# A four-layer graph network on one core: eight blocks' sums placed by node instead of by feature, and a third gathered tile in every run

## The reference, cut to what matters

```python
for l in range(4):
    m = relu(x[src] + (edge_weight @ We[l] + be[l]))       # one row of 512 per edge
    agg = segment_sum(m, dst, 1250)
    h = ((1 + eps[l]) * x + agg) @ W1[l] + b1[l]
    h = relu(batchnorm(h) * gamma[l] + beta[l])            # mean and variance over the nodes
    x = relu(h @ W2[l] + b2[l])
out = layernorm(x0 + x)
```

## Time and profile before

| | us |
|---|---|
| median of 3 runs | 1293.48 |
| lowest, highest | 1288.86, 1293.76 |
| profiled execution | 1292.47 |
| its span, first to last instruction | 1290.6 |
| PE busy | 1208.2 (94%) |
| DVE busy | 1035.8 (80%) |
| POOL busy | 783.6 (61%) |
| ACT busy | 553.5 (43%) |

### The profile page before, as it was taken

One profiled execution on the slowest core, in us unless ns is written; L12 is line 12 of the kernel. 1 busy time (PEld: TensorE's weight loads), 2 busy tenths in 40 slices (PEclk: granted clock), 3 DMA queues, 4 the chain that ended last, 5 costly groups with the idle time before them and its releaser, 6 DMA issues.

```text
span 1290.6 us, 26518 instructions
## 1 busy us (share of the span) xinstructions
PE 1208.2 (94%) x7483; PEld 771.6 (60%) x7483; DVE 1035.8 (80%) x2134; ACT 553.5 (43%) x1159; POOL 783.6 (61%) x831
## 2 busy tenths in 40 slices
PE   2887999999999999999998999999998999999997
PEld 2884566666655566666654566665554566666653
DVE  7978888888876978887776978887767888888777
ACT  1923344434364444434355444444345434343343
POOL 0055677677706777777715777777714777777720
PEclk9558899999999999999999999999999999999999
DMA  3156677677736777777746777777745777777752
GB/s 113 56 186 194 193 205 218 197 209 211 232 111 200 216 218 216 217 217 218 235 136 199 215 217 217 217 217 217 234 146 185 215 217 217 218 216 215 221 190 107
DMA packets 92578, 254.23 MB, mean 197 GB/s; under 512 B 19902, under 2 KB 23114, under 8 KB 92428
## 3 DMA queue, kind: packets, MB, share of 16 engines
q0 software_dynamic: 65600, 215.01, 56.5%
q1 hardware_dynamic: 25804, 36.42, 8.6%
q10 hardware_dynamic: 1024, 1.05, 0.3%
HBM read 239.24 MB, written 12.97 MB: 195 GB/s over the span
## 4 chain that ended last, share of the span: by engine, by line
POOL 42%; PE 29%; issue 15%; DVE 10%; DMA 2%; ACT 0%; ACTq 0%; DVEq 0%; POOLq 0%
POOL rows L827 42%; PE y_ps L2106 10%; PE y_ps L1985 6%; PE pair_ps L1932 4%; DVE rows L1543 3%; DVE rows L1429 2%; PE h_ps L2063 1%; PE y_ps L2117 1%; DMA rows<-node_table,src_fast 1%; PE h_ps L1858 1%; DVE src_onehot L1360 1%; PE uT_ps L2016 1%; DMA node_table<-rows 1%; PE pair_ps L2049 1%; PE uT_ps L2023 1%
## 5 line engine op out<-in xcount | busy, mean ns | idle before, releaser
L827 POOL DMA_INDIRECT rows<-node_table,src_fast x820 | 780.9, 952 | 453.3 <-issue 248.2
L1543 DVE SCALAR_TENSOR_TENSOR rows<-We_ps,negw_fast,rows 128x512 f32<-128x512 f32 x820 | 566.3, 744 | 81.6 <-DMA rows<-node_table,src_fast 81.2
L1985 PE MATMUL y_ps<-table_parts,src_onehot 128*128 128x512 f32 x1664 | 428.7, 409 | 22.0 <-DVE table_parts L637 8.0
L1985 PEld LDWEIGHTS y_ps<-table_parts,src_onehot 128*128 128x128 f32 x1664 | 291.3, 190 | 191.2 <-issue 88.0
L1003 ACT ACTIVATE rows<-y_ps 128x512 f32<-128x512 f32 x416 | 248.7, 598 | 217.7 <-PE y_ps L1985 207.2
L1932 PE MATMUL pair_ps<-rows,onehot 128*32 128x512 f32 x2504 | 306.2, 601 | 15.0 <-DVE rows L1543 14.8
L1360 DVE TENSOR_TENSOR src_onehot<-y_ps,src_bc 126x256 fp32r<-126x256 f32 x376 | 150.8, 417 | 64.2 <-PE y_ps L1985 63.9
L1932 PEld LDWEIGHTS pair_ps<-rows,onehot 128*32 128x32 f32 x2504 | 67.4, 109 | 149.5 <-issue 112.2
L2063 PEld LDWEIGHTS h_ps<-uT,W_sb 128*128 128x128 f32 x1152 | 135.5, 194 | 6.1 <-issue 3.4
L2063 PE MATMUL h_ps<-uT,W_sb 128*128 128x128 f32 x1152 | 136.4, 278 | 0.0
L2106 PE MATMUL y_ps<-rows,hT 128*128 128x512 f32 x288 | 124.5, 594 | 0.0
(11 more groups left out here) (251 smaller groups left out, 793.3 us busy)
## 6 DMA issues: line engine op xcount, KB each, us to landing
late_rows<-node_table SPq DMA_DIRECT2D x1536, 2.0 KB
rows<-node_table,src_fast POOLq DMA_INDIRECT x820, 3.7
b_bc<-node_table ACTq DMA_DIRECT2D x512, 2.0 KB
node_table<-rows SPq DMA_DIRECT2D x29, 256.0 KB, 3.6
src_onehot<-near_ws SPq DMA_DIRECT2D x416, 2.0 KB
x_now<-x_pad SPq DMA_DIRECT2D x10, 512.0 KB, 7.7
W_sb<-W SPq DMA_DIRECT2D x4, 1024.0 KB, 5.5
rows<-W SPq DMA_DIRECT2D x16, 256.0 KB
```

The source lines that it names most:

```text
L827: nc.gpsimd.indirect_dma_start(rows[:, slot, :], None, table[:, :], bass.IndirectOffsetOnAxis(src_fast[:, t:t + 1], 0)).then_inc(landed[q] ...
L1543: last = nc.vector.scalar_tensor_tensor(rows[:, slot, :], We_ps[:, :], negw_fast[:, t:t + 1], row, ALU.mult, ALU.max)
L1985: last = nc.tensor.matmul(y_ps[k % 2][:, :], src_onehot[:, 2 * (k % ONEHOTS) + b, :], table_parts[:, part, 2 * pair_of(k) + b, :], start=( ...
```

## The change

Two things. First, for blocks 0 to 7 (`BY_NODE` = 8) the sums are placed by node: the placing one-hot is the weight, in pieces of 128x32, and all 512 columns of `pair_sb` or `carry` stream through (`place_block`, six matmuls, five in block 0), at quad 1 where the old placing stood. VectorE adds the result to `u` (`add_sums`, after its messages of quad 3), and TensorE transposes the whole `u` (`turn_block`, after the sums of quad 3). ScalarE's copies move: `keep_carry` after `block_placed`, `finish_block` after `turn_block`, `scale_u` from before the near tiles to the middle of them. `place_w` of layer 0 moves from quad 1 to quad 2. Blocks 8 and 9 are placed as before.

Second, `EXTRA_RUNS[1]` takes every fourth run from 7 on instead of every eighth from 11, so that all later runs have three near tiles: 108 tiles a layer instead of 104 (one more in steps 1, 3, 5 and 7), and 20 extras instead of 16 at the start. `ln_stats` and `ln_mv` become parts of `stats`.

```diff
-    EXTRA_RUNS = [slice(LONG_A_STEP + 1, LONG_RUNS, LONG_A_STEP), slice(2 * LONG_A_STEP + 3, LONG_RUNS, 2 * LONG_A_STEP)]
-    TWO_RUNS = slice(LONG_A_STEP + 3, LONG_RUNS, 2 * LONG_A_STEP)
+    EXTRA_RUNS = [slice(LONG_A_STEP + 1, LONG_RUNS, LONG_A_STEP), slice(LONG_A_STEP + 3, LONG_RUNS, LONG_A_STEP)]
...
             def scale_u(n, i):
-                if n:
-                    act.wait_ge(u_turned, n)
+                if i == BLOCKS - 1:
+                    act.wait_ge(u_turned, n // BLOCKS * (BLOCKS - BY_NODE) + i - BY_NODE)
+                elif n:
+                    act.wait_ge(block_summed, n + 1)
...
                         act.wait_ge(We_rows, 64 * (l + 1))
+                    if 0 < i <= BY_NODE:
+                        act.wait_ge(block_placed, BY_NODE * l + i)
+                        keep_carry()
                     if 0 < i:
                         finish_block(n - 1)
-                        nc.scalar.copy(carry[:, :], pair_sb[:, 1, :]).then_inc(carry_copied, 1)
-                    if i < BLOCKS - 1:
+                    if i > BY_NODE:
+                        keep_carry()
+                    if i == 0:
                         scale_u(n, i)
                     copy_pair(0, n, quad_summed[3], n + 2)
                     for q in range(0 if i else 3, 4):
                         make_tiles(l, first + q)
+                        if q == 1 and i < BLOCKS - 1:
+                            scale_u(n, i)
...
+            def add_sums(n, l, i):
+                dve.wait_ge(u_ready, n + 1)
+                dve.wait_ge(block_placed, BY_NODE * l + i + 1)
+                nc.vector.tensor_tensor(u[:, :], node_sums, u[:, :], ALU.add).then_inc(u_whole, 1)
...
+                        if q == 3 and 0 < i <= BY_NODE:
+                            add_sums(n - 1, l, i - 1)
...
                     sum_quad(q, l, i)
+                    if q == 3 and 0 < i and not final:
+                        turn_block(n - 1, l, i - 1)
...
+                        if not final and q == 1:
+                            place_block(n - 1, l, i - 1)
...
-                    if q == 1 and l == 0 and not final:
+                    if q == (2 if i else 1) and l == 0 and not final:
                         place_w(i)
...
+            def place_block(n, l, i):
+                pe.wait_ge(uT_copied, n + 1)
+                pe.wait_ge(place_ready, n + 1)
+                pe.wait_ge(pair_copied[0], n + 2)
+                pe.wait_ge(pair_copied[1], n + 2)
+                if i:
+                    pe.wait_ge(carry_copied, (BLOCKS - 1) * l + i + 1)
+                nodes = [slice(g * WIN, (g + 1) * WIN) for g in range(P // WIN)]
+                for g in range(PLACED // WIN):
+                    nc.tensor.matmul(node_sums[nodes[g], :], place0(i)[:, nodes[g]], pair_sb[:, 0, :],
+                                     start=True, stop=g == 1 or g == 0 and not i)
+                nc.tensor.matmul(node_sums[nodes[3], :], place1(i, WIN, 2 * WIN), pair_sb[:, 1, :], start=True, stop=True)
+                if i:
+                    nc.tensor.matmul(node_sums[nodes[0], :], place1(i - 1, HALF, PLACED), carry[:, :],
+                                     start=False, stop=True)
+                nc.tensor.matmul(node_sums[nodes[2], :], place1(i, 0, WIN), pair_sb[:, 1, :],
+                                 start=False, stop=True).then_inc(block_placed, 1)
+
+            def turn_block(n, l, i):
+                pe.wait_ge(u_whole, BY_NODE * l + i + 1)
+                for c in range(C):
+                    last = nc.tensor.matmul(uT_ps[:, c, :], u[:, c * P:(c + 1) * P], ident[:, :],
+                                            start=(c == 0), stop=True, is_transpose=True, skip_group_check=True)
+                last.then_inc(block_summed, 1)
```

More of the change, by code:

```diff
@@ L53, in gnn_layers @@
     QUADS = STEP // 4
+    BY_NODE = BLOCKS - 2
     EPS = 1e-05
@@ L362, in gnn_layers @@
         bn_bias = sb("bn_bias", [P, C])
-        ln_stats = sb("ln_stats", [P, BLOCKS, 6])
-        ln_mv = sb("ln_mv", [P, BLOCKS, 2])
+        ln_stats = stats[:, 0, 0:BLOCKS, :]
+        ln_mv = stats[:, 1, 0:BLOCKS, 0:2]
         ln_std = sb("ln_std", [P, BLOCKS])
@@ L477, in gnn_layers @@
         u_turned = sem("u_turned")
+        block_placed = sem("block_placed")
+        u_whole = sem("u_whole")
         u_ready = sem("u_ready")
@@ L540, in rest_of_last @@
             return y_ps[TILES_A_LAYER % 2][:, 0:D // 2].rearrange("p (c n) -> p c n", n=P)
+        node_sums = turned_uT
         def sums_of(c, l, i):
@@ L605, in placings @@
                     (EXTRA_RUNS[1], slice(7, 8), last[:, rest_lanes(EXTRA_RUNS[1]), 0:1]),
-                    (TWO_RUNS, slice(2, 6), first[:, rest_lanes(TWO_RUNS), :]),
-                    (TWO_RUNS, slice(6, 8), last[:, rest_lanes(TWO_RUNS), :]),
                     (FIRST_RUNS, slice(2, 5), first[:, early_lanes, 0:3]),
@@ L984, in slow_scale_u, with keep_carry @@
                                      ACT.Identity, scale=eps1[:, 0:1]).then_inc(u_scaled, 1)
+            def keep_carry():
+                nc.scalar.copy(carry[:, :], pair_sb[:, 1, :]).then_inc(carry_copied, 1)
             def copy_pair(h, n, summed, value):
@@ L1953, in edge_step @@
                     if 0 < i:
-                        if q == (0 if final else 1):
+                        if final and q == 0:
                             open_block(n - 1, l, i - 1, True)
                             add_first_pair(n - 1, l, i - 1)
-                        if q == 1:
+                        if final and q == 1:
                             close_block(n - 1, i - 1)
+                        if not final and q == 1:
+                            place_block(n - 1, l, i - 1)
                         if q == (2 if final else 3):
```

## The result

The kernel after took 1310.34 us (median of 4 runs, 1308.94 to 1310.96), the kernel before 1291.41 us beside it (4 runs, 1288.86 to 1293.76): ratio 1.0133, interval 1.0100 to 1.0167. The forecast was 1284 us, faster, in a range from 1277 to 1296; the kernel is slower by 1.3%, outside that range.

What follows compares the result with a forecast made beforehand. GpSimd's gathers were taken to bound layers 1 to 3, TensorE close behind. Start +12.05, layers 1 to 3 -15.0 and layer 0 -6.0 gave -9.0 us: 1283.5 from 1292.47, median 1284 us, range 1277 to 1296.

Steps and rivals of the forecast that it cites:

- Part 2: Layers 1 to 3: four gathers fewer each save 5.0 us a layer, -15.0 us, if GpSimd still sets the end.
- Part 2's other condition: Layers 1 to 3: TensorE must keep up with 12 near tiles every step; spare 1.7, 0.0 and 1.3 us.
- Part 1: Start: four more extras at 3.01 us each, unhidden, add 12.05 us; bounds +9 and +13 us.
- Part 3: Layer 0: its steps shorten to 26.3 us, some 6.0 us saved in all; bounds 0 and 10.2 us.
- The placing: TensorE, each block: six matmuls take 1.85 us (1.39 at best) instead of 2.72, gaining 0.87 us.
- Rival 3: VectorE comes late to `add_sums`, TensorE stands at `turn_block`: +14.5 us, 1308 us; chance 0.08.
- Rival 2: Layers 1 to 3: TensorE becomes the bound through new gaps, losing 10.7 of 15.0 us: 1295 us; chance 0.18.

Runs made afterwards that it cites:

- experiment 4: Kernel after, with SyncE loading eight row numbers at a time into registers, every second tile, instead of four: 1285.73 us, ratio 0.9959.
- experiment 5: Kernel before with 108 tiles, 20 extras and SyncE loading eight row numbers at a time, placing by feature kept: 1290.02 us, ratio 0.9979.
- SP eight: Edit used in several runs: SyncE loads eight row numbers a piece, every second tile, instead of four; on the kernel after 1285.73 us.
- experiment 6: Kernel before with only SyncE's eight row numbers at a time added: 1291.22 us, ratio 0.9982.
- Experiment 1: Kernel after with the old runs put back (104 tiles, 16 extras), so placing by node alone: 1289.54 us, ratio 0.9983.
- experiment 8: Kernel after with SyncE's eight row numbers at a time, plus three idle products after each of the last 11 extras: 1293.77 us, ratio 1.0018.

## Why the prediction was wrong

**The step that failed** is one sentence of Part 2: "SP's four more loads of weight rows a layer are paced by the tiles and cost nothing." It has the dependence the wrong way round. The loads are not paced by the tiles alone: in SyncE's program each of them stands behind a piece of `late_rows`, so a tile costs SyncE a round of 2.28 us. The prediction asked which engine is next after GpSimd, took TensorE (25.46 us a step on the mean) and left SyncE out, whose 11.5 x 2.28 = 26.2 us was already the largest of the three. It could have been read from the trace of before, by the timeline of SyncE's queue, and the waits gave a sign: TensorE already waited nine times for weight rows, 4.6 us. Nothing of it shows in the page's busy times, where issuing is not counted, nor in the chain of before, where GpSimd set the pace. The -15.0 us of Part 2 came out as +13.8. With SyncE out of the way (experiment 4) the three layers give -2.8, -5.5 and -4.1, -12.3 us in all: the size of the term was nearly right, its condition was not.

Part 2's other condition, that the new placing must let TensorE keep up step by step, was not needed. In experiment 5, with the old placing and TensorE as the bound, the three layers give -4.9, -5.1 and -3.6, -13.6 us in all. What placing by node adds with 108 tiles and SP eight is in layer 0: 300.34 us in experiment 4, 306.11 in experiment 5.

The Trainium skill, "Perfetto Trace Analysis", section "What "DMA-bound" means", names the issuing engine's sequencer as a bound of its own, seen as a track solid with DMA slices. The bound agrees with this trace, the sign only in part: issues of DMAs fill 1.24 + 0.25 of SyncE's 2.28 us, and most of the rest is the register load (0.57 us). The Trainium skill, "DMA: Bandwidth & Descriptors", section "Issuing engines are not separate DMA queues", says that the time to initiate a DMA is usually small beside the DMA. That holds for the single load here, 0.25 us to issue against 2.79 to land; and yet the round of five issues and a register load, not the landing, set the time.

**Part 1, the start, was right.** The extras' sums before took 12.05 us. In the chains of two kernels with 20 and 16 extras under the same clock all the way (experiments 5 and 6) they are 24.00 and 12.05 us, 11.95 apart; the forecast was 12.05. The row of experiment 5:

```profile
75.80 24.00 PE h_ps L1855 x112
```

In the profile after they are

```profile
75.19 20.89 PE h_ps L1880 x112
```

since part of them ran at full clock in that execution (below), which is why the start shows +8.6 and not +12. Experiment 1, with 16 extras and such a stretch, has 8.93 us: 11.96 apart again.

**Part 3, layer 0, was right.** Steps 2 to 6 took 26.30 to 26.41 us; 26.3 was forecast, and the chain there (195 to 250 us) goes over ScalarE's DMA issues and `next_w` to `place_w`, as the forecast had it. Layer 0 gave -5.1 us of -6.0. There SyncE has 27.4 us a step too, and its lead fell from 17.7 us (tile 18) to 2.6 (tile 101): TensorE waited for weight rows once in these steps, 0.4 us, and the layer ended before it became more.

**The placing** cost a little less than I took. Of the 3.43 us from the end of the sums of quads 0 and 1 (630.18 us) to `turn_block` (633.61), quads 2 and 3 have 1.85, which leaves 1.58 us for six matmuls, between my 1.39 and 1.85. TensorE's timeline of an earlier block shows how the half-filled round went:

```profile
575.02 0.61 PE L2065 MATMUL uT_ps<-pair_sb,place 128*32 128x512 f32 x3
...
575.45 0.59 PE L2069 MATMUL uT_ps<-carry,place 128*32 128x512 f32 x1
575.45 0.62 PE L1954 MATMUL pair_ps<-rows,onehot 128*32 128x512 f32 x1
575.46 0.59 PE L2071 MATMUL uT_ps<-pair_sb,place 128*32 128x512 f32 x1
575.47 0.62 PE L1954 MATMUL pair_ps<-rows,onehot 128*32 128x512 f32 x1
```

A set of products starts every 0.43 us, one to each group of 32 partitions, and two products of quad 2 start beside the placing's second round. The Trainium skill, "TensorEngine Tiling (Array Packing)", section "Tiling Modes", says that different tiles can load weights and multiply in parallel; these starts agree. Still, 3.43 us are eight such sets, where the 28 products of placing and quads would fill seven: not all the room in the half-filled round was won back. A step of 12 tiles without a gap is 24.92 us instead of 25.94, a gain of 1.02 us against 0.87.

**The rivals.** Rival 3 gave 1308 us, near the 1310 measured, by a mechanism that is false: VectorE does wait for the placing before `add_sums` (41.9 us in 29 waits in the kernel after) and TensorE's weight loads wait for that sum, but neither reaches TensorE's products. Rival 2's sign, gaps on TensorE in layers 1 to 3, came true with another cause. None of the four named SyncE, and so the range was built from bounds on the wrong engines.

**What stays open.** Ten or twelve runs of one kernel spread by 5 to 8 us (experiment 6: 1286.94 to 1294.76). The stretch of full clock at the start moves it by some 3 us; where the rest comes from was not tried.

## What to carry to other kernels

Before saying which engine is next, write down for every engine and every queue that issues DMAs what one turn of its loop takes, and hold it against the step: a queue has no busy share on the page, so read it from its timeline (here 12 x 2.28 us against a step of 25). Where a queue runs ahead, look how its lead changes over a layer: a lead that falls from 13 us to 3, as in the kernel before, is a bound that has hardly struck yet, and half a tile more a step made it strike. If it does, shorten the turn before giving up the change: here half as many register loads turned 1.0133 into 0.9959.

## What the runs showed of the hardware

- Issuing with addresses from registers has a fixed part here: loading four row numbers took 0.55 to 0.60 us (L651 in the chain above), loading eight 0.79 us (the median in experiment 4), and a row's move and issue 0.32 us (2.56 / 8 in experiment 4), for rows of 2 KB.
- TensorE's clock at the start differs from one execution to the next. In the kernel before it was granted 0.50 (1.2 GHz) through all the extras' sums; in the kernel after it was 1.00 (2.4 GHz) from 75.62 to 79.04 us, at the head of sums that keep TensorE busy from 75.19 on, and 0.50 again behind, with TensorE busy all the while:

```profile
71.77:75.62 3.85, 3.85 (x20) 3.51 (x18) 3.81 (x8) 1.65 (x16) 1.27 (x1) 0.50 0.71 251
75.62:79.04 3.42, 3.42 (x32) 3.42 (x33) 2.92 (x4) 2.92 (x10) 2.81 (x3) 1.00 0.60 168
79.04:96.17 17.13, 17.13 (x83) 17.13 (x82) 6.26 (x7) 0.00 (x0) 13.47 (x13) 0.50 0.77 248
```

  It is worth 3.1 us of the start (24.00 - 20.89). More products did not bring it back in experiment 8, where TensorE was busy 41.49 of 44.37 us at 0.50. Why it comes in some executions and not in others was not found.
